# Cross-attention and expert block: per-head keys and queries, scores as pairs of 64-row matmuls

## The reference

```
q  = LN(latents) @ Wq ;  k, v = split(concat(LN(ctx), LN(latents)) @ Wkv)      # latents = LN(x)
for each of 16 heads (64 wide), each of 4 batches:
    attn = softmax(q @ k.T / 8)            # 256 queries x 512 keys
    out  = attn @ v
x = x + LN(concat(out) @ Wout)
xn = LN(x)
h_e = silu(xn @ W_up[e]) ;  y_e = h_e @ W_down[e]      # 64 experts, 64 wide
x = x + silu(xn @ Ws_up) @ Ws_down + sum_e cw[e] * y_e # cw: top 8 of 64, normalised sigmoids
```

## Time and profile before

| what | value |
|---|---|
| median of three runs | 410.69 us |
| time of the profiled execution | 407.39 us |
| its span | 405.6 us |
| mean granted TensorE clock, share of full | 0.964 |
| opening, until the values are done | 0 to 62.6 us |
| attention steps, until the last score tile is masked | 62.9 to 255.6 us |
| from there to the start of the experts | to about 302 us |
| experts | to 405.6 us |

### The profile page before, as it was taken

One profiled execution on the slowest core, in us unless ns is written; L12 is line 12 of the kernel. 1 busy time (PEld: TensorE's weight loads), 2 busy tenths in 40 slices (PEclk: granted clock), 3 DMA queues, 4 the chain that ended last, 5 costly groups with the idle time before them and its releaser, 6 DMA issues.

```text
span 405.6 us, 7755 instructions
## 1 busy us (share of the span) xinstructions
PE 362.5 (89%) x2353; PEld 283.6 (70%) x2353; DVE 295.9 (73%) x700; ACT 267.3 (66%) x539; POOL 257.4 (63%) x347
## 2 busy tenths in 40 slices
PE   3578978999999999999999999732799999999996
PEld 2456755888888888888888888521566777777774
DVE  2788787786777768677686877538677777778895
ACT  3768886857768677686867767603586666666681
POOL 4214133869789788878878878723126777766691
PEclk9999999999999999999999999965599999999999
DMA  7300041797977999699696799940000000000001
GB/s 240 84 0 2 0 78 22 126 159 138 183 131 126 172 137 190 109 138 175 113 182 123 134 153 142 161 116 0 2 0 2 0 0 0 0 0 0 2 0 52
DMA packets 121123, 34.38 MB, mean 85 GB/s; under 512 B 110977, under 2 KB 120705, under 8 KB 121089
## 3 DMA queue, kind: packets, MB, share of 16 engines
q1 hardware_dynamic: 120656, 32.39, 45.7%
q10 hardware_dynamic: 432, 1.57, 1.2%
HBM read 8.26 MB, written 0.52 MB: 22 GB/s over the span
## 4 chain that ended last, share of the span: by engine, by line
PE 71%; ACT 8%; DVE 8%; DMA 6%; POOL 4%; issue 3%; SPq 0%; DVEq 0%; POOLq 0%; ACTq 0%
PE ps L712 15%; PE ps L714 15%; PE ps L713 15%; PE ps L811 8%; PE ps L845 4%; DMA pT<-p 4%; PE ps L826 4%; PE ps L953 4%; PE ps L837 3%; DMA tok<-in_ctx 2%; POOL p L393 2%; DVE v L1216 2%; ACT v L576 2%; POOL p L391 2%; ACT prob L546 1%
## 5 line engine op out<-in xcount | busy, mean ns | idle before, releaser
L393 POOL TENSOR_TENSOR p<-prob,p 128x512 f16<-128x512 f32 x96 | 111.8, 1165 | 7.7
L1171 DVE CUSTOM_DVE_ANT_0 sc<-ps,mask_add 128x512 f32<-128x512 f32 x128 | 85.7, 688 | 30.6 <-PE ps L714 29.7
L546 ACT ACTIVATE prob<-sc,p_bias 128x512 f32<-128x512 f32 x128 | 91.5, 716 | 4.1 <-POOL p L393 2.0
L391 POOL CAST p<-prob 128x512 f16<-128x512 f32 x96 | 58.6, 610 | 51.5 <-ACT prob L546 35.8
L554 ACT ACTIVATE p_bias<-neg_max,ln_range 128x2 f32<-128x2 f32 x64 | 18.5, 290 | 52.8 <-DVE neg_max L1171 52.8
L1368 DVE TENSOR_TENSOR h<-h,ps 128x1024 f32<-128x1024 f32 (+1 forms) x32 | 39.1, 1221 | 19.0 <-PE ps L953 17.8
L811 PE MATMUL ps<-pT,v 128*64 128x256 f16 x768 | 47.6, 273 | 3.8 <-issue 3.8
L712 PE MATMUL ps<-kv_hi,q_hi 128*128 128x512 f32 x128 | 50.5, 395 | 0.1
L714 PE MATMUL ps<-kv_hi,q_lo 128*128 128x512 f32 x128 | 50.2, 392 | 0.0
L713 PE MATMUL ps<-kv_lo,q_hi 128*128 128x512 f32 x128 | 50.0, 391 | 0.0
L811 PEld LDWEIGHTS ps<-pT,v 128*64 128x64 f16 x768 | 42.1, 110 | 4.3 <-issue 4.3
(11 more groups left out here) (197 smaller groups left out, 785.0 us busy)
## 6 DMA issues: line engine op xcount, KB each, us to landing
wup_s<-in_L_ffn_W_up SPq DMA_DIRECT2D x8, 256.0 KB, 3.4
wdn_s<-in_L_ffn_W_down SPq DMA_DIRECT2D x8, 256.0 KB, 3.8
pT<-p SPq DMA_TRANSPOSE x96, 3.1
wkv_s<-in_L_xattn_Wkv ACTq DMA_DIRECT2D x2, 512.0 KB, 7.0
x_in<-in_x SPq DMA_DIRECT2D x2, 256.0 KB, 8.1
wq_s<-in_L_xattn_Wq ACTq DMA_DIRECT2D x1, 512.0 KB, 7.6
tok<-in_ctx SPq DMA_DIRECT2D x4, 128.0 KB, 8.1
wo_s<-in_L_xattn_Wout SPq DMA_DIRECT2D x1, 512.0 KB, 5.1
```

What stands on the lines that cost most here:

```text
L391: pool.tensor_copy(p16[:, t, 0, :], prob[:, t, :]).then_inc(s_phi, 1)
L393: pool.tensor_tensor(p16[:, t, 1, :], prob[:, t, :], p16[:, t, 0, :], ALU.subtract).then_inc(s_plo, 1)
L546: act.activation(prob[:, t, :], sc[:, t, :], ACT.Exp, bias=p_bias[:, t:t + 1], scale=-1.0, accum_out=p_sum[:, i % 2, t:t + 1]).then_inc(s_ ...
L1171: return dve.tensor_tensor_reduce(sc[:, t, :], ps[:, SCORE_BANK + (i * TILES + t) % SCORE_BANKS, :], mask_add[:, i % B, :], -SCALE, -LEAST ...
```

## The change

Keys are now projected: for each step, `keys` makes k of both heads of the pair (128 rows: two heads of 64) for one batch, in a bank of its own, and `queries` makes q of both heads for two batches, once in two steps. Scores are then the product of 64 rows of k with 64 rows of q, and the two heads of a pair stand in the upper and the lower 64 rows. `scores(i, qt)` issues the two heads in turn, term by term, into two banks, so a step has two such pairs with six matmuls each where it had four tiles with three each. Both waits of a pair stand ahead of its first matmul. Score tiles and the spread sums now take turns in the three banks (`turns`, five turns in a step, four in the first two). The products of Wq and Wk are gone, and with them their transposes and splits; instead Wk and Wq are split (POOL makes the low halves).

A step's place is now half of the batches first: batches 0 and 1 for all eight pairs (16 steps), then batches 2 and 3. So the first half of the projected output can be taken after step 15 (`evac_out(0)` in ACT's iteration 19), one bank serves both halves, and the small loads behind `s_late` go out on SP after the transposes of step 20. `spread_inverse` stands behind `attend` instead of ahead of it. In the opening the chunks of v have four banks until chunk 13 and three from chunk 14, the first scores come a pair at a time, and the load of the value weights goes first.

The diff, cut to what the steps above use:

```diff
--- before.py
+++ after.py
+        def step(i):
+            return i // (STEPS // 2), i % (STEPS // 2) // 2, 2 * (i // (STEPS // 2)) + i % 2
+
+        turns = [(what, i, t) for i in range(STEPS + 2)
+                 for what, t in [("score", t) for t in range(TILES) if i < STEPS] + [("spread", 0)]
+                 if what == "score" or i >= 2]
+        turns = [(what, i - 2 if what == "spread" else i, t) for what, i, t in turns]
+
+        def turn_bank(*what):
+            return SCORE_BANK + turns.index(what) % SCORE_BANKS
+
+        def turn_before(*what):
+            n = turns.index(what) - SCORE_BANKS
+            return turns[n] if n >= 0 else None
...
-            return (0, 1)[n % 2] if n < 8 else (0, 1, 6, 7)[n % 4]
+            return (0, 5, 3, 4)[n % 4] if n < 14 else (0, 5, 6)[n % 3]
...
-        between = {1: ["t2"], 2: ["m1"], 3: ["t3", "m2"], 5: ["m3"], 7: ["q0"], 8: ["q1"], 9: ["q2"], 10: ["q3"], 13: ["s0"], 14: ["s1"],
-                   16: ["s2", "b0"], 17: ["x0", "x1"], 18: ["s3", "b2"], 20: ["x2"], 22: ["x3"]}
+        between = {1: ["t2"], 3: ["t3"], 9: ["k0"], 10: ["q0"], 12: ["k1"], 14: ["s0"], 15: ["b0"], 16: ["x0", "x1"], 17: ["s1"],
+                   18: ["b2"], 20: ["x2"], 22: ["x3"]}
...
+            def load_late():
+                sp.wait_ge(s_av, STEPS // 2)
+                sp.dma_start(x_res[:, :, :], x.rearrange("b (q p) d -> p (b q) d", p=P)).then_inc(s_late, 16)
...
+                if i == STEPS // 2 + 4:
+                    load_late()
...
-            def q_high(c, quarter, bank=Q_BANK):
...
+            def k_high(i):
+                act.wait_ge(s_k, i + 1)
+                act.activation(k_hi[:, i % 2, :], ps[:, K_BANK, :], ACT.Copy).then_inc(s_khi, 1)
+
+            def q_high(j):
+                act.wait_ge(s_q, j + 1)
+                act.activation(q_hi[:, j % 2, :], ps[:, Q_BANK, :], ACT.Copy).then_inc(s_qhi, 1)
...
             for i in range(1, STEPS):
-                if 2 <= i <= STEPS - B + 1:
-                    q_high(i + 2, (i - 2) % B)
+                if i == STEPS // 2 + 3:
+                    evac_out(0)
+                if i + 1 < STEPS:
+                    k_high(i + 1)
+                    if i % 2 == 1:
+                        q_high((i + 1) // 2)
                 shift_range(i, 0)
...
-            def scores(i, t):
-                b = i % B
-                head, qt = t // QT, t % QT
-                at = b * S + qt * P
-                three(ps[:, SCORE_BANK + (i * TILES + t) % SCORE_BANKS, :], q_hi[:, head, at:at + P], q_lo[:, head, at:at + P],
-                      kv_hi[:, b, :], kv_lo[:, b, :]).then_inc(s_score, 1)
+            def keys(i):
...
+                if i:
+                    pe.wait_ge(s_klo, i)
+                three(ps[:, K_BANK, :], wk_hi[:, cut], wk_lo[:, cut], kv_hi[:, b, :], kv_lo[:, b, :]).then_inc(s_k, 1)
...
+            def scores(i, qt):
+                at = i % 2 * S + qt * P
+                for head in range(2):
+                    follow(turn_before("score", i, 2 * qt + head))
+                for n, (a, c) in enumerate(((q_hi, k_hi), (q_hi, k_lo), (q_lo, k_hi))):
+                    for head in range(2):
+                        rows = slice(head * DH, (head + 1) * DH)
+                        mm = pe.matmul(ps[:, turn_bank("score", i, 2 * qt + head), :], a[rows, i // 2 % 2, at:at + P],
+                                       c[rows, i % 2, :], start=(n == 0), stop=(n == 2), skip_group_check=True)
+                        if n == 2:
+                            mm.then_inc(s_score, 1)
+
+            def follow(earlier):
+                if earlier is None:
+                    return
+                what, i, t = earlier
+                if what == "score":
+                    pe.wait_ge(s_masked, i * TILES + t + 1)
+                else:
+                    pe.wait_ge(s_rbsb, i + 1)
...
+            clear_out()
+            keys(2)
+            queries(1)
             for i in range(1, STEPS + 2):
                 if i < STEPS:
-                    for t in range(TILES):
-                        score_step(i, t)
+                    pe.wait_ge(s_klo, i + 1)
+                    pe.wait_ge(s_qlo, i // 2 + 1)
+                    scores(i, 0)
+                    scores(i, 1)
                 if i <= STEPS:
                     turn_last(i - 1)
                 if i >= 2:
+                    attend(i - 2)
                     spread_inverse(i - 2)
-                    attend(i - 2)
                 if i >= 3:
                     project(i - 3)
-                if i <= STEPS - B:
-                    if i == 1:
-                        pe.wait_ge(s_qlo, B)
-                    else:
-                        pe.wait_ge(s_rbsb, i - 1)
-                    queries((i + 3) // B, (i - 1) % B)
+                if i + 2 < STEPS:
+                    keys(i + 2)
+                    if i % 2 == 0:
+                        queries(i // 2 + 1)
...
                 mask_scores(i, 0)
                 mask_scores(i, 1)
-                if 2 <= i <= STEPS - B + 1:
-                    q_low(i + 2, (i - 2) % B)
+                if i + 1 < STEPS:
+                    k_low(i + 1)
                 mask_scores(i, 2)
                 mask_scores(i, 3)
                 if i >= 2:
                     take_inverse(i - 2)
+                if i + 1 < STEPS and i % 2 == 1:
+                    q_low((i + 1) // 2)
                 invert(i - 1)
                 last_low(i - 1)
```

More of the change, by code:

```diff
@@ L751, in _ @@
-            head_matrices(2)
-            head_matrices(3)
-            def queries(pair, quarter, bank=Q_BANK):
-                head, half = quarter % 2, quarter // 2
-                rows = slice(2 * half, 2 * half + 2)
-                three(ps[:, bank, :].rearrange("p (b s) -> p b s", b=2),
-                      w_all[:, pair, head, :], w_all[:, pair, 2 + head, :],
-                      kv_hi[:, rows, S:2 * S], kv_lo[:, rows, S:2 * S]).then_inc(s_q, 1)
-            def scores(i, t):
-                b = i % B
-                head, qt = t // QT, t % QT
-                at = b * S + qt * P
-                three(ps[:, SCORE_BANK + (i * TILES + t) % SCORE_BANKS, :], q_hi[:, head, at:at + P], q_lo[:, head, at:at + P],
-                      kv_hi[:, b, :], kv_lo[:, b, :]).then_inc(s_score, 1)
+            def keys(i):
+                half, pair, b = step(i)
+                cut = slice(pair * P, (pair + 1) * P)
+                if i == 0:
+                    pe.wait_ge(s_wklo, 1)
+                    pe.wait_ge(s_kvlo, 2)
+                if i == STEPS // 2:
+                    pe.wait_ge(s_kvlo, B)
+                if i:
+                    pe.wait_ge(s_klo, i)
+                three(ps[:, K_BANK, :], wk_hi[:, cut], wk_lo[:, cut], kv_hi[:, b, :], kv_lo[:, b, :]).then_inc(s_k, 1)
@@ new lines, in queries @@
+            def queries(j):
+                half, pair, b = step(2 * j)
+                cut = slice(pair * P, (pair + 1) * P)
+                if j == 0:
+                    pe.wait_ge(s_wqlo, 1)
+                else:
+                    pe.wait_ge(s_qlo, j)
+                three(ps[:, Q_BANK, :].rearrange("p (b s) -> p b s", b=2), wq_hi[:, cut], wq_lo[:, cut],
+                      kv_hi[:, b:b + 2, S:2 * S], kv_lo[:, b:b + 2, S:2 * S]).then_inc(s_q, 1)
+            def scores(i, qt):
[9 more added lines that the diff above has]
+                            mm.then_inc(s_score, 1)
@@ L784, in _ @@
                     transpose_tokens(n)
+                elif what == "k":
+                    keys(n)
                 elif what == "q":
[L786 to L791 removed]
+                    queries(n)
                 elif what == "s":
                     if n == 0:
[L794 to L796 removed]
+                        pe.wait_ge(s_klo, 1)
+                        pe.wait_ge(s_qlo, 1)
+                        pe.wait_ge(s_vlo, 11)
+                    else:
+                        pe.wait_ge(s_vlo, 12)
                     scores(0, n)
             def attend(i):
[L801 removed]
+                half, pair, b = step(i)
                 for t in range(DMA_TILES):
@@ L843, in project, with clear_out @@
                 pe.wait_ge(s_ao, i + 1)
-                pair, at = i // B, i % B * S
-                pe.matmul(ps[:, OUT_BANK + at // 512, at % 512:at % 512 + S], wo_s[:, pair, :], ao[:, :],
+                half, pair, b = step(i)
+                if i == STEPS // 2:
+                    pe.wait_ge(s_outT, 1)
+                    clear_out()
+                at = i % 2 * S
+                pe.matmul(ps[:, OUT_BANK, at:at + S], wo_s[:, pair, :], ao[:, :],
                           start=False, stop=False, skip_group_check=True).then_inc(s_wout, 1)
+            def clear_out():
+                pe.matmul(ps[:, OUT_BANK, :], zeros16[:, 0:P], zeros16[:, :], start=True, stop=True)
             def turn_out(half, bank):
```

188 lines of the change are left out of this document (64 added, 124 removed).

## The result

The changed kernel took 428.43 us (median of four runs, 427.53 to 430.29) against 410.18 us for the kernel before in the same comparison: a ratio of 1.048, interval 1.044 to 1.052. It is slower, inside the range, and 7.4 us slower than the 421.0 forecast.

The account below looks back on a forecast made before the run. PE's instructions, one behind another, were taken to bound the steps at 6.41 us. Attention +13.1, opening -0.8 and end -2.0 gave +10.3 on 410.69, so 421.0 us; range 412 to 443.

Parts of the forecast that it names:

- The wait: Each step: second score pair waits for its own step's first mask, PE idle 1.1 us; pairs save 0.13, not 1.38.
- The size of a step: Attention steps 3 to 28: 6.48 and 7.17 in turn, mean 6.82 us, 0.41 longer than before.
- the sum: Whole kernel: attention +13.1, opening -0.8, end -2.0, together +10.3 us.
- Pairs at 0.23, loads in the shadow: Score matmuls: two heads' 64-row halves run side by side, 0.23 us a pair; concurrent pairs with the wait, chance 0.68.
- serial halves: Rival, score pairs: halves run one after the other, 0.46 a pair, 36 us more, 457 us; chance 0.10.
- the loads' pace: Rival, score pairs: weight loads take 0.38 per pair; 445 us, half overlapped 433; chance 0.12.
- the hidden wait: Rival, steps: second pair follows the first at once, step 5.6, 386 us; chance 0.10 with any other gain.
- Changes of form: PE's array switching between 128, 64-row and 64-column form: two more per step, 0.1 us each, bounds 0 to 0.4 a step.
- just in time: DVE in steps with the late spread: free at 7.55, when PE's next first tile is ready; 0.7 early in the others.
- Opening: Before step 1's scores: banks -1.7, one split -0.7, keys and queries +1.6; sum -0.8 us, bounds -3.9 and +1.3.
- I take no loss: Granted clock: PE busy some 83% in steps, and 81% from 25 to 62.5 us had kept 1.00, so no loss.
- End: After the attention: early small loads let POOL add the bias sooner, -2.0 us; wait before last attend left, bounds -1.5 and +0.5.

## Why the prediction was right, and where it was short

*The wait: right, and shown.* The sign hung on the step that the second pair waits for the mask of its own step, for 1.1 us in each. The trace has 31 waits of 1.06, and filling them gave back 0.87 us a step.

*The size of a step: 7.06, not 6.82.* This is 6.2 of the 9.8 us that the sum fell short in the profiled execution. (The median fell short by 7.4 only, because the sum put it 3.3 above that execution and it was 0.9 above; that is luck.) The mask was put at T + 1.07 by the terms of a steady step; from the first to the second term of the pair it is 0.34, not 0.23, so T + 1.18. This is not the 64 rows' own. The tile of 128 rows that waited in the earlier trace rows of the kernel before shows it too, 0.33:

```profile
69.31 0.50 PE L712 MATMUL ps<-kv_hi,q_hi 128*128 128x512 f32 x1
69.64 0.39 PE L713 MATMUL ps<-kv_lo,q_hi 128*128 128x512 f32 x1
```

The sum had it in the 0.80 of the second pair and left it out of the first. The restart was put at 0.75 after the mask's start, from the earlier trace rows; it took 0.85 (156.77 to 157.62). In the kernel with heads one after the other it is 0.75 (154.45 to 155.20), so the restart of a pair is dearer than that of a tile; why stays open. From the turned tile to the next step, with queries, the forecast was 4.45 (7.17 less 2.62 and one change of form) and 4.47 were measured.

*Pairs at 0.23, loads in the shadow: right.* The rivals of serial halves and of the loads' pace fell, as did the hidden wait. The Trainium skill ("TensorE: Matmul & The Clock Gate", Part 3: Packing small matmuls) has matmuls in distinct row groups run concurrently, and the rows agree: 0.23 for two, and still so where the heads were issued one after the other.

*Changes of form: the gap right, what follows it missed.* I took 0.1 per change. The first score starts 0.32 after the last keys' term (155.27 to 155.59) and the turned tile 0.36 after the last score (158.15 to 158.51), where 0.23 is usual: 0.09 and 0.13. The Trainium skill's rule that a change of mode drains the engine ("TensorEngine Tiling (Array Packing)", Tiling Modes, Key Properties) agrees with these two gaps. The 0.11 ahead of the second term, missed in the first pair, comes on top: entering the 64-row form costs 0.20 in all, but that part stands without a change too.

*VectorE: right that it costs nothing.* Moving the spread changed nothing. It was not just in time, though, but had room: it stood idle 0.37 ahead of a first mask behind a split of queries and 1.68 ahead of the other (156.77 and 164.17), where the forecast had 0 and 0.7.

*Opening: wrong, +1.8 instead of -0.8, beyond its bound of +1.3.* The keys and queries ahead of T(1) were right: from VectorE's last value to T(1) it is 1.77 now and was 0.32, 1.45 more for a forecast of 1.6. The miss is in the values, which end 0.4 later (62.96 against 62.59) where the count of banks and splits had 2.4 earlier. The count left out things that the trace shows. ScalarE's table load and two exponentials stood together ahead of chunks 17 and 18, so VectorE and TensorE stood 2.65 and 2.44 us; and the clock fell behind that. "I take no loss" for the clock was a step that failed: it went by the busy share, 83% to come and 81% in the opening before, and in the steps, with 85%, 1.00 was right; in the opening it was not. And the first value chunks came at half the pace, 0.43 a matmul until 27.5, where those of the kernel before came at 0.23; there TensorE had multiplied Wq and Wk until 22.9, here it had stood 5.17 us. How the loss divides is shown by single executions only: moving the exponential took T(1) from 64.73 to 64.40, and that opening at full clock ended at 62.60, which leaves -0.3 against the kernel before. The fall at 72 us is most of the miss in steps 1 and 2: in the kernel with the moved exponential, at 1.00 there, T(1) to T(3) took 12.13, against the forecast's 12.1.

*End: right within 0.6 us,* -1.4 for -2.0. The stretch up to the last attend gave the 1.5 that had been left as a bound, but not by TensorE's wait alone, which went from 3.79 to 3.30. GpSimd's last split ends 9.14 us after T(31) instead of 10.05 (282.58 + 1.15, and 260.45 + 1.16 in the earlier trace rows), and the last attend starts 4.01 behind it instead of 4.57. That the early loads would be covered was right too, as steps 21 and 22 show.

## What to carry to other kernels

Count a saving in slots only where the engine has no wait to put them into: if two results go out as one unit, the unit waits for the later of their buffers, and with few buffers that can be a consumer of the same step. Then look for work that can stand in that wait before buying another buffer: here two moved calls were worth 20 us, and a fourth bank no more than they. And don't take the clock as granted from a busy share: here the same opening kept it in one execution and lost it in another, and 1.8 us went with it.

## What was not expected of the hardware

Two heads in different rows of the array ran side by side even when all three matmuls of one were issued ahead of the other's. And a tiny VectorE instruction beside a large GpSimd subtract can be stretched to nearly its length, here in the opening of the changed kernel (it takes 0.16 or 0.17 alone):

```profile
13.39 2.34 POOL L400 TENSOR_TENSOR wk_lo<-wkv_s,wk_hi 128x1024 fp32r<-128x1024 f32 x1 [4.25 <-ACT wk_hi L528]
13.44 2.30 DVE L1123 SCALAR_TENSOR_TENSOR shift<-mv,rs 128x4 f32<-128x4 f32 x1
...
24.57 2.37 POOL L402 TENSOR_TENSOR wq_lo<-wq_s,wq_hi 128x1024 fp32r<-128x1024 f32 x1 [8.85 <-ACT wq_hi L540]
...
25.07 1.90 DVE L1161 TENSOR_SCALAR range_v<-range_v 128x2 int32<-128x2 int32 x1
```

When both subtracts were moved earlier, another tiny instruction met them and took 2.24. Not every one is hit: three of 128x1 that started inside the second subtract, from 24.63 to 24.89, took 0.14 or 0.15. What decides it stays open.
